# Attention scores from two row strips of 34, a fourth seeded bias and a new order of the first step

## What is computed

```python
Q, K, V = proj(layernorm(x), Wq, bq), proj(ctx, Wk, bk), proj(ctx, Wv, bv)
scores = einsum('bhid,bhjd->bhij', Q, K) / sqrt(8) + m[h] * softplus(1000 + |i - j|)
x = x + (softmax(scores) @ V) @ Wo.T + bo
z = layernorm(x)
probs = softmax(z @ Wr); cw = the two largest of probs, else 0
x = x + sum_e cw[:, e] * ((silu(z @ Wg[e]) * (z @ Wu[e])) @ Wd[e]) + (silu(z @ Sg) * (z @ Su)) @ Sd
```

## Time and profile before

| | |
|---|---|
| median of 3 runs | 241.05 us (240.48 to 241.5) |
| profiled execution | 241.2 us |
| its span, first to last instruction | 239.4 us |
| mean granted TensorE clock | 0.986 |
| PE busy | 217.2 us, 91% |
| DVE busy | 174.7 us, 73% |
| ACT busy | 119.0 us, 50% |
| POOL busy | 75.4 us, 31% |

### The profile page before, as it was taken

One profiled execution on the slowest core, in us unless ns is written; L12 is line 12 of the kernel. 1 busy time (PEld: TensorE's weight loads), 2 busy tenths in 40 slices (PEclk: granted clock), 3 DMA queues, 4 the chain that ended last, 5 costly groups with the idle time before them and its releaser, 6 DMA issues.

```text
span 239.4 us, 6083 instructions
## 1 busy us (share of the span) xinstructions
PE 217.2 (91%) x1942; PEld 177.2 (74%) x1942; DVE 174.7 (73%) x610; ACT 119.0 (50%) x283; POOL 75.4 (31%) x180
## 2 busy tenths in 40 slices
PE   2989387888999999999999999999999989989995
PEld 2667244676789788887888787887897779868985
DVE  4689504699579966996799678967896689654791
ACT  8475423647443654366336633574446434753420
POOL 2510002401193109410770068014900390029000
PEclk9999959999999999999999999999999999999999
DMA  5553566032704170144314340335032700160000
GB/s 155 164 93 103 133 162 233 4 100 51 175 1 104 52 181 17 57 95 124 77 43 103 92 107 4 96 96 149 3 101 58 191 0 4 50 154 1 1 25 22
DMA packets 13079, 20.24 MB, mean 85 GB/s; under 512 B 2800, under 2 KB 9440, under 8 KB 12544
## 3 DMA queue, kind: packets, MB, share of 16 engines
q1 hardware_dynamic: 12624, 18.77, 30.3%
q10 hardware_dynamic: 432, 1.19, 1.5%
HBM read 16.03 MB, written 3.78 MB: 83 GB/s over the span
## 4 chain that ended last, share of the span: by engine, by line
PE 46%; issue 29%; POOL 10%; DVE 5%; DMA 4%; ACT 3%; SPq 0%; DVEq 0%; POOLq 0%; ACTq 0%
PE ps_m L549 9%; PE ps_up L523 8%; POOL hid L1315 6%; PE ps_pv L456 5%; PE ps_st L437 4%; PE ps_up L528 4%; DVE nmax L975 3%; PE ps_pv L463 3%; PE ps_s L379 2%; DMA stacks_sb<-qk_dram 2%; PE ps_st L491 2%; PE ps_st L397 1%; DMA ident<-in_c_ident 1%; PE ps_m L478 1%; ACT probs L747 1%
## 5 line engine op out<-in xcount | busy, mean ns | idle before, releaser
L799 ACT ACTIVATE th<-ps_up 128x256 f32<-128x256 f32 x72 | 27.7, 384 | 39.0 <-PE ps_up L528 38.5
L747 ACT ACTIVATE probs<-ps_st 128x512 f32<-128x512 f32 x64 | 36.8, 592 | 16.9 <-PE ps_st L437 16.7
L549 PE MATMUL ps_m<-wd_sb,hid 128*128 128x128 f32 x288 | 44.8, 283 | 0.0
L975 DVE TENSOR_REDUCE nmax<-ps_s 128x4 f32<-128x512 f32 x64 | 42.0, 680 | 0.8 <-issue 0.4
L1079 DVE SCALAR_TENSOR_TENSOR tg<-th,ps_up 128x256 f32<-128x256 f32 x72 | 29.7, 413 | 13.3 <-ACT th L799 12.5
L1315 POOL TENSOR_TENSOR hid<-hid,crep 128x256 f32<-128x256 f32 x56 | 39.1, 729 | 0.2 <-issue 0.2
L549 PEld LDWEIGHTS ps_m<-wd_sb,hid 128*128 128x128 f32 x288 | 37.6, 191 | 1.0
L1085 DVE TENSOR_TENSOR hid<-tg,ps_up 128x256 f32<-128x256 f32 x72 | 29.7, 412 | 1.0
L523 PE MATMUL ps_up<-x_hi,wg_hi 128*128 128x256 f32 x72 | 26.6, 369 | 0.4 <-ACT x_hi L780 0.2
L437 PE MATMUL ps_st<-stacks_sb 98*128 98x128 f16 x256 | 25.6, 224 | 0.4 <-DMA stacks_sb<-nmT 0.3
L1279 POOL TENSOR_TENSOR ve<-mv,eps_sb 128x1 f32<-128x1 f32 x16 | 3.0, 191 | 71.5 <-DVE mv L1026 71.5
(11 more groups left out here) (147 smaller groups left out, 446.6 us busy)
## 6 DMA issues: line engine op xcount, KB each, us to landing
crep<-cw_dram SPq DMA_DIRECT2D x28, 256.0 KB, 4.6
stacks_sb<-qk_dram SPq DMA_DIRECT2D x32, 128.0 KB, 3.3
qk_dram<-qk_parts SPq DMA_DIRECT2D x16, 128.0 KB, 1.8
out_y<-x_all SPq DMA_DIRECT2D x8, 128.0 KB, 4.6
wg_sb<-in_wgT ACTq DMA_DIRECT2D x1, 576.0 KB, 3.5
wu_sb<-in_wuT ACTq DMA_DIRECT2D x1, 576.0 KB, 3.3
wd_sb<-in_wd SPq DMA_DIRECT2D x1, 576.0 KB, 4.9
x_all<-in_x SPq DMA_DIRECT2D x2, 256.0 KB, 3.3
```

Source lines behind the costliest of these rows:

```text
L549: last = mm(ps_dn[:, b * P:(b + 1) * P], hid[:, buf, c, b * P:(b + 1) * P], wd_sb[:, c, :], start=(c == 0 and b == 0), stop=(c == SHARED), ...
L747: fn(probs[:, b, g * HG * P:(g + 1) * HG * P], scores_bank(a, g)[:], ACT.Exp).then_inc(exp_sb, 1)
L799: fn(th[:, c % 2, :], ps_up[c % 2][:, 0, :], ACT.Tanh, scale=0.5).then_inc(tanh_sb, 1)
L975: v.tensor_reduce(nmax[:, b, HG * g:HG * g + HG], ps_s[g % 2][:].rearrange("p (h j) -> p h j", h=HG), AX_X, ALU.max, negate=True).then_inc ...
```

## The change

1. **Strips.** `stacks_sb` holds heads 0 to 7 in rows 0 to 33 and heads 8 to 15 in rows 64 to 97 (32 rows and two for ones and maxima). The pads and their filling go. Each stack row is read by twice as many DMAs of half the size (eight instead of four for a step), and `shift_rows` issues two instead of one.
2. **Groups.** Groups are taken in the order 0, 2, 1, 3, so that they alternate between the strips. `scores` and `scores_T` take a tuple of groups. Most are still taken one by one; two at once, head by head in alternation, are the first two of `scores` for b = 0, and the second and third of `scores_T` for b = 1.
3. **Seeds.** The group with three bias matmuls (now third, i = 2) is seeded for both b: for b = 0 by ACT, in `seed_second`, behind the first exponential. All seeds go to bank `ps_st1`. DVE's second seed waits for the first exponential of b = 1. `scores_T` 0 of b = 1 goes ahead of `down` 8.
4. **First step.** Both shift rows are sent ahead of `write_parts(1)`; the two `qk_low` move into the row maxima of b = 1; some `keep_clock` counts change.
5. **Tail.** DVE instead of POOL weighs chunks 2 and 3 of group 6, and `down` takes these ahead of `expert_in_T`.

```diff
-AROWS = ZROWS + 2
+AROWS = SROWS + 2
+HS = H // 2
+ORDER = (0, 2, 1, 3)
...
-        stacks_sb = sb("stacks_sb", [AROWS, 2, 2, H, T], F16)
+        stacks_sb = sb("stacks_sb", [STRIP + AROWS, 2, 2, HS, T], F16)
...
                 for row in (0, 2 * DH):
-                    src = bass.AP(qk_dram.tensor, buf * 5 * (P * T), [[H * T, 2 * DH], [1, H * T]])
...
+                    for s in range(2):
+                        src = bass.AP(qk_dram.tensor, (buf * 5 * P + s * HS) * T, [[H * T, 2 * DH], [1, HS * T]])
+                        at = STRIP * s + row
+                        sp.dma_start(stacks_sb[at:at + 2 * DH, buf, 0].rearrange("r h t -> r (h t)"), src).then_inc(s_stack, 16)
...
-                if at_start(a): shift_rows(a, 0, abuf)
+                if at_start(a):
+                    shift_rows(a, 0, abuf)
+                    shift_rows(a, 1, abuf)
                 if p is not None: write_parts(p, 1 - abuf)
                 if not at_start(a): shift_rows(a, 0, abuf)
                 if p is not None: stack_k(p, 1 - abuf)
-                shift_rows(a, 1, abuf)
+                if not at_start(a): shift_rows(a, 1, abuf)
...
+                seeded = {i: not at_start(a) and i % 2 == 0 for i in groups}
...
+                for k in range(HG):
+                    for i in groups:
+                        row, h = STRIP * (i % 2), HG * (i // 2) + k
+                        last = mm(scores_bank(a, i)[:, k * P:(k + 1) * P], ks[buf][row:row + AROWS, h, b * P:(b + 1) * P],
+                                  qs[buf][row:row + AROWS, h, b * P:(b + 1) * P], start=first[i], stop=True,
+                                  skip_group_check=True)
...
+            def seed_second(a):
+                act.wait_ge(exp_sb, 2 * NHG * a + 1)
+                fn(ps_st[1][:], bias_T[:, 1, :], ACT.Copy).then_inc(seed0_sb, 1)
...
-                dve.wait_ge(exp_sb, 2 * NHG * a + NHG + g - 1)
-                v.tensor_copy(ps_st[(g + 1) % 2][:], bias_T[:, g, :]).then_inc(seed1_sb, 1)
+                dve.wait_ge(exp_sb, 2 * NHG * a + NHG - 1 + 2 * g)
+                v.tensor_copy(ps_st[1][:], bias_T[:, g, :]).then_inc(seed1_sb, 1)
...
             down(f - 1, (0, 1), 1 - last, f)
-            keep_clock(6, ps_st[1][:, 0:P])
+            down(f - 1, (2, 3), 1 - last, by_dve=2)
             expert_in_T(f)
```

More of the change, by code:

```diff
@@ L354, in project_v, with scores @@
                 last.then_inc(v_mm, 1)
[L356 to L362 removed]
+            def scores(a, b, groups, buf):
+                n = 2 * NHG * a + NHG * b
+                if b == 0 and 0 in groups:
+                    pe.wait_ge(s_stack, 128 * a + 128)
                     if at_start(a):
@@ L433, in scores_T @@
                         pe.wait_ge(act_pads, 2)
[L434 to L440 removed]
+                    elif isinstance(a, int) and a == 1:
+                        pe.wait_ge(act_pads, 4)
+                first = {i: False if seeded[i] else bias(scores_bank(a, i), ORDER[i])[0] for i in groups}
+                for k in range(HG):
+                    for i in groups:
+                        row, h = STRIP * (i % 2), HG * (i // 2) + k
+                        last = mm(scores_bank(a, i)[:, k * P:(k + 1) * P], ks[buf][row:row + AROWS, h, b * P:(b + 1) * P],
+                                  qs[buf][row:row + AROWS, h, b * P:(b + 1) * P], start=first[i], stop=True,
+                                  skip_group_check=True)
+                        first[i] = False
+                        if k == HG - 1:
+                            last.then_inc(st_mm, 1)
             def weigh_values(a, b, f=None):
@@ L1102, in first @@
                 max_low(0, 0)
-                for g in range(NHG):
-                    row_max(0, 1, g)
+                row_max(0, 1, 0)
+                row_max(0, 1, 1)
+                qk_low(1, 1)
+                qk_low(1, 0)
+                row_max(0, 1, 2)
+                row_max(0, 1, 3)
                 max_high(0, 1)
                 max_low(0, 1)
-                qk_low(1, 1)
-                qk_low(1, 0)
                 weights_low()
@@ L1352, in _ @@
             run_steps(pool, step)
-            for pair in range(1, PAIRS):
+            for pair in range(2, PAIRS):
                 weigh_experts(NG - 2, pair, (NG - 2) % 2)
```

229 lines of the change are left out of this document (106 added, 123 removed).

## The result

The changed kernel took 254.26 us (median of four runs, 251.81 to 257.69), the kernel before 240.95 beside it. The runs of the changed kernel fall in two groups, near 251.8 us with a mean granted clock of 0.98 and near 257 us with one of 0.946 to 0.953, and the comparisons in this document leave the second group out: the ratio is **1.0447, with a 95% interval from 1.0417 to 1.0476**, or 251.8 us. The same kernel in a second session gave 1.0407 (1.0352 to 1.0462). The direction was forecast; the amount was 3.2 us too small against 251.8.

What follows compares the result with a forecast made beforehand. Middle steps were taken as bound by PE's own issue, the start by a DMA chain, the tail by PE. 241.2 + 10.5 (seven steps) - 2.3 (start) - 0.75 (tail) = 248.6 us; range 245 to 252, 8 in 10: 241 to 254.

Steps and rivals of the forecast that it cites:

- The price of a block: In each step, a block of strip matmuls between full ones costs PE 0.25 us; +3.2 us a step.
- rivals A and B: Whole kernel: A, strips change nothing on PE, 232.4 us, chance 0.15; B, a step loses only 0.4 us, 241, chance 0.10.
- The pairs: In each step, two pairs of groups run strip beside strip, saving PE 0.22 us each, 0.44 in all.
- The fourth seed: Group 1 of b=0: ACT's copy replaces three bias matmuls, saving PE 0.38 us a step and costing nothing on ACT.
- The order: b=1, `scores_T` 0 ahead of `down` 8: 0.44 + 1.0 us of PE's work hides DVE's seed for group 2; costs nothing.
- What waits absorb: In a middle step, existing PE waits take up 0.9 us of the 2.4 us added.
- The start: First step: both shift rows go ahead of other traffic and the clock stays at 2.4 GHz, against later loads: -2.3 us.
- The tail: Chunks 2 and 3 of `down` go ahead of `expert_in_T`, where PE ran idle transposes: -0.75 us.
- Rival D: First step: the start doesn't pay, as loads are late by what shift rows gained: 251 us; chance 0.64 together with the forecast.
- C: Steps: pairs don't overlap and POOL is held, delaying norm2 and `expert_in_T`: 2.3 to 2.6 us a step, 255; chance 0.11.

Runs made afterwards that it cites:

- experiment 5: The changed kernel with its two pairs taken one group after the other: 251.4 and 251.8 us; ratio 1.0499, which takes in a third run of 254.6.
- experiment 4: The fourth seed undone, in the changed kernel without strips: 239.5 us; and in the changed kernel with strips: ratio 1.0412, 250.4 to 252.4 us.

## Why the prediction was right, and where it was short

**The price of a block: right.** 0.25 forecast; 0.09 + 0.12 + 0.03 measured, and the entrance is the same 0.21 behind an `up` for 32 and for 34 rows, which rules out rivals A and B. The forecast came from two rows of another kind, a 48-row f32 pair and a narrow transpose, because both showed the same 0.10 at the entrance. That it carried over to f16 strips is what the runs bore out.

**The pairs: the overlap right, its worth only in part.** 0.22 was forecast for each and is measured for the first (experiment 5). The second overlaps as well, its two groups' first starts 3 ns apart. But in after `values_T` follows its last start after 0.336 us, where the exit takes 0.145, so 0.19 of its 0.22 is waited for. The forecast rested on sixteen matmuls in column tiles as the nearest row. The Trainium skill, page "TensorE: Matmul & The Clock Gate", Part 3, gives about 4 ns between starts in different row groups; the trace has 3 to 4.

**The fourth seed: mis-sized.** Forecast -0.38 a step, measured -0.15. The three bias matmuls did leave TensorE, but 0.2 of the 0.39 is now waited for at `scores_T` 0 of b=1 (experiment 4); without strips the copy is a loss of 0.14.

**The order: the step that failed.** I wrote that `scores_T` 0 is moved ahead of `down` 8 and that PE's work hides the seed. That looked at the seed for group 2 alone. `scores_T` 0 has a seed of its own, which in the kernel before ended while `down` 8 ran, about 0.1 us ahead of its reader (156.49 + 0.69 to 157.27 in that step); moving the reader past its cover costs 0.2 us a step without strips, where with smaller waits behind it the order comes to +0.36. In after the same 0.2 is waited for, but only together with the fourth seed: with strips and three seeds TensorE comes late enough. So the "nothing" and the whole 0.38 of the seed were wrong by one and the same wait.

**What waits absorb: mis-sized the other way.** 0.9 was forecast for after. The strips cost 1.49 a step of 2.76 (3.2 - 0.44), so 1.3 was free, the 0.2 for DVE's seed among it. These three misses nearly cancel, which is luck: +0.36 and +0.23 against -0.37. A step became 1.7 longer, not 1.5.

**The start: right in size, half wrong in its reasons.** -2.3 forecast, -2.46 in after, -2.8 in the kernel before. `scores_T` of b=1 began at 28.84 (28.4 forecast), wd was issued at 35.18 (35.5). Its scaling ended at 41.6 as forecast, but by luck: wd had landed at 39.4 and not at 40.4, and ACT came to it only at 40.46, behind work that waited for x. The clock did not stay at 2.4 GHz to the end of the step (half from 40.7 on), and the idle stretch that counts is not near 27 but one of 2.15 us ahead of L480, for x:

```profile
28.84 0.38 PE L397 MATMUL ps_st<-slope_hi,dist 128*128 128x512 f16 x1 [1.05 <-ACT probs L752]
...
38.61 0.33 PE L480 MATMUL ps_m<-ident,attn 128*128 128x128 f32 x1 [2.15 <-DVE attn L1017]
```

I had followed wd through SP's queue and not x, two places ahead of it.

**The tail: wrong.** -0.75 forecast, 0 measured (+0.3 ahead of `expert_in_T`, -0.3 behind). I took the end of the products (217.5) for the start of `expert_in_T`, and forgot that the two chunks themselves stand between.

**The clock in the second step: not forecast at all.** I put it at about 1.4 us from the kernel with the pairs one by one (3.1 in the first interval less the 1.6 of its other steps), which was at half for 6.8 us there; no run takes the drop away by itself.

The misses can be added up for the 251.42 us of the kernel with the pairs one by one, 2.8 above the 248.6: steps 7 x 1.63 = 11.4 where 10.5 were forecast, 0.9; clock 1.4; tail 0.45 (0.3 gained by the ends of the table, 0.75 forecast; its 0.3 ahead of `expert_in_T` is in the steps); start 0. Against the 251.8 of after it is 3.2. Rival D is out, since the start paid by 2.5, and for C the overlap was not missing, and POOL's products show no wait of note (0.2 us in all between 100 and 230 us of after). The range of 241 to 254 holds 251.8; the median over all runs, 254.26, lies just above it.

**The version that beats both** keeps the start and the tail and leaves strips, order and fourth seed alone: 237.2 us, ratio 0.984 to before, some 14 us below the changed kernel.

## What to carry to other kernels

A matmul that uses another part of the array than its neighbours costs TensorE about 0.1 us at the entrance and 0.1 at the exit, whatever the length of the block. Here a block of four small matmuls has 0.22 us of work of its own, so between full ones the two changes double it; longer blocks would spread the price, which no run here tried. When a consumer is moved ahead in a list, look for every producer that the skipped work was covering, its own first, and look again after every other saving, since a saving further up can bring the wait back. And where a load is late, list all loads in the queue behind and ahead of it: freeing one hands the wait to the next.

## What the runs showed of the hardware

- The change of shape costs 0.09 to 0.10 us at the entrance with 32, 34, 48 and 64 rows (48 in f32, the others in f16), and 0.09 to 0.12 at the exit.
- Two groups on different row strips overlap even when the program gives them one behind the other: second strip's first start 14 ns after the first's, the fourth matmul of the first group as seventh start. No interleaving by hand was needed.
- Four profiles of strip kernels show the 2.4 GHz clock lost a second time, for 3.4 to 10.2 us between 51 and 66 us, with PE busy nearly all of it (6.71 of 6.90 us with the pairs one by one, 9.76 of 10.24 with idle transposes, 3.42 of 3.42 with the old start); 21 idle transposes in the one long idle stretch of the first step did not prevent it. Two runs of the strip kernel with three seeds had at most some 3.5 us at half in all, so it does not come in every execution.
